# Recurrent layer and FP4 feed-forward layer on one core: the last two tiles' feed-forward middle in three column parts, and the end of four engines' programs as lists

## The chip, the core and the metric

The kernel runs on one core of one Trainium2 chip. The metric is the device time of one execution in microseconds (us). The kernel before took 566.85 us (median of 3 runs, 566.63 to 566.96).

## What is computed

The input x has 4 sequences of 2048 rows of 256 numbers, fp32. Two layers follow one another, each with a residual sum and a layer norm:

```python
# first layer: linear recurrence with a state of 16 numbers, then a norm with gamma and beta
xB = einsum('bsh,nh->bsn', x, B);  xD = einsum('bsh,oh->bso', x, D)
state = state @ A.T + xB_t                      # for every step t
out = layernorm(states @ C.T + xD) * gamma + beta
x = layernorm(x + out)
# second layer: gated feed-forward, 704 inner columns; every operand is quantized to FP4
# in blocks of 16 along its last dimension (scale = max|block| / 6) and dequantized
gate = fp4_linear(x, w_gate);  y = fp4_linear(x, w_up)
h = silu(gate) * y
x = layernorm(x + fp4_linear(h, w_down))
```

The output is x, again 4 x 2048 x 256.

## The kernel before

The 8192 rows are 64 tiles of 128 rows, numbered 0 to 63. In the code (h, m) is tile 8h + m. A prologue builds the states of the recurrence and quantizes the weights; then every tile goes through the same chain over five engines. Matmuls in fp32 are made of three passes over operands that are split into a high and a low part (`split_products`, line 1434), hence names such as htHi and htLo.

The chain of one tile, with the engine and the line: `layer` (TensorE, L1434 into yb), `mean_square` (ScalarE, L713), `ve1`, `pow1` (POOL, L534), `scale_gamma` and `add_x` (VectorE), `nm2`, `sq2`, `ve2`, `pow2`, `nr2`, `norm2` (L808); then the quantization of x1: `x_max` (L1062), `x_scale` (VectorE, L1067), `x_recip` (L1072), `x_norm` (POOL, L544), `x_abs` (ScalarE, L741), `x_sum`, `x_grid` (VectorE, L1077 and L1083), `x_scale` (POOL, L549), `x_turn` (TensorE transposes, L1460), `x_hi` (ScalarE, L754), `x_lo` (VectorE, L1088, writes xtLo). The gate and up products `gu0`, `gu1`, `gu2` (TensorE, L1434, into the three banks of gu, 512 + 512 + 384 columns) are next. The feed-forward middle is `silu_gate` (ScalarE, L758), `times_up` (VectorE, L1095, the product), `h_max` (L1099), `h_scale` and `h_recip` (L1104 and L1109), `h_norm` (POOL, L560), `h_abs` (ScalarE, L777), `h_sum` and `h_grid` (VectorE, L1126 and L1133), `h_scale` (POOL, L571 and L575), `h_turn` (six transposes, L1517), `h_hi` (ScalarE, L788), `h_lo` (VectorE, L1147), and the down projection `ffn_down` (17 matmuls, L1434, L1540, L1541). At the end of the chain stand `add_x1` (VectorE, L1154), `nm3` (L728), `sq3` (L735), `ve3` (L720), `pow3` (POOL, L534), `nr3` (L801), `norm3` (ScalarE, L817) and the store by SP.

Every engine runs its program in order, and semaphores tie them together: an instruction waits until a counter has reached its tile's number. The order of each program comes from `run`: a list of steps with lags, where step (op, lag) works in pass i of the loop on the tile i - lag:

```python
run(act, [(norm3, 11), (nm3, 9), (sq3, 9), (nr2, 3), (norm2, 3), (t_hi, 0), (h_hi, 7), (h_abs, 6),
          (silu_gate, 5), (nm2, 2), (x_hi, 4), (sq2, 2), (nr3, 10), (ve2, 2), (mean_square, 1),
          (x_abs, 3), (ve1, 1), (ve3, 9)], FILLED["act"])
run(dve, [(x_grid, 2), (scale_gamma, 0), (x_max, 1), (add_x, 0), (x_scale, 1), (h_lo, 5), (x_recip, 1),
          (h_sum, 4), (times_up, 3), (h_grid, 4), (x_lo, 2), (h_max, 3), (add_x1, 5), (h_scale, 3),
          (x_sum, 1), (h_recip, 3)], FILLED["dve"])
run(pe, [(h_turn, 6), (gu1, 4), (gu2, 4), (x_turn, 3), (layer, 0), (ffn_down, 6), (gu0, 3)], FILLED["pe"])
```

`run` writes a hardware loop over h = 2 to 7 and behind it the remaining passes (tiles that are still under way), in the same order. So the loop of each engine ends at another tile: ScalarE's last silu in the loop is that of tile 58, VectorE's last product in the loop that of tile 60, TensorE's last `gu0` in the loop that of tile 60.

At the end, tile 63 alone has its middle in two halves (`is_last`, `halves`, 384 + 320 columns) from `h_norm` on, and TensorE has four idle matmuls with the identity ahead of some steps (`unread(4, ...)`, L1293, twenty in all), which nothing reads. The down projections of the last five tiles write one half-bank, yb[:, 0:256], so each waits for the `add_x1` of the tile before.

## Time and profile before

| what | value |
| --- | --- |
| median of 3 runs | 566.85 us |
| the profiled execution | 566.68 us |
| its span, first to last instruction | 564.9 us |
| TensorE (PE) busy | 551.6 us, 98% |
| VectorE (DVE) busy | 518.0 us, 92% |
| POOL busy | 494.4 us, 88% |
| ScalarE (ACT) busy | 468.3 us, 83% |
| mean granted TensorE clock | 0.998 |

The profile is of one execution. Times of instructions are counted from the start of the span; the 1.8 us between span and execution lie around it. Busy times of TensorE count overlapping matmuls once. An instruction that is next in line overlaps the one before by about 0.1 us in the records. In the timelines the bracket behind a row gives the idle time of the engine before it and what ended it; the granted clock is a share of 2.4 GHz.

### The profile page before, as it was taken

The numbers are of one execution on the slowest core, as the hardware profiler recorded it, in microseconds if no ns is written. First come the engines' busy times: TensorE is split into PE (matmuls) and PEld (weight loads), VectorE is DVE, ScalarE is ACT, GpSimd is POOL, SyncE is SP. The second block draws the span as 40 slices with busy tenths as digits, with TensorE's granted clock in tenths as the row PEclk, the third lists the DMA queues.
The fourth block names the chain that finished last, engine by engine and source line by source line (L and its number), as shares of the span: only waits on it lengthen the run. The fifth ranks groups of instructions, "written<-read, shape, count | busy, mean of one in ns | idle before, by whom it ended". The sixth has DMA issues, their size and how long they took to land.

```text
span 564.9 us, 12830 instructions
## 1 busy us (share of the span) xinstructions
PE 551.6 (98%) x3751; PEld 495.0 (88%) x3751; DVE 518.0 (92%) x1241; ACT 468.3 (83%) x1415; POOL 494.4 (88%) x674
## 2 busy tenths in 40 slices
PE   9899999999999999999999999999999999999995
PEld 7577779999999999999999999999999999999894
DVE  4896799999999999999999999999999999999973
ACT  3557867889888998988889898888989888898756
POOL 2566887999999999999999999999999999998653
PEclk9999999999999999999999999999999999999999
DMA  8951000011121111111211111121111122100001
GB/s 291 383 182 30 5 24 24 22 41 47 56 61 60 52 60 58 49 50 59 59 52 56 58 50 50 59 59 55 54 59 49 50 59 59 56 22 19 20 20 46
DMA packets 35772, 36.25 MB, mean 64 GB/s; under 512 B 6752, under 2 KB 34464, under 8 KB 34720
## 3 DMA queue, kind: packets, MB, share of 16 engines
q1 hardware_dynamic: 35744, 35.90, 20.1%
q8 instruction: 14, 0.23, 0.2%
q14 instruction: 14, 0.11, 0.1%
HBM read 19.50 MB, written 8.39 MB: 49 GB/s over the span
## 4 chain that ended last, share of the span: by engine, by line
PE 90%; DVE 5%; ACT 2%; issue 1%; POOL 0%; POOLq 0%; DVEq 0%; ACTq 0%
PE gu L1434 41%; PE turned L1434 18%; PE yb L1434 8%; PE turned L1517 7%; PE turned L1460 2%; PE yb L1448 1%; PE grid L1293 1%; PE turned L1541 1%; PE turned L1540 1%; PE gu L1345 1%; PE yb L1345 1%; DVE scratch L1095 1%; DVE scratch L1133 1%; PE gu L1381 1%; PE turned L1381 1%
## 5 line engine op out<-in xcount | busy, mean ns | idle before, releaser
L1434 PE MATMUL gu<-wguHi,xtHi 128*128 128x512 f32 (+1 forms) x384 | 151.3, 394 | 0.4 <-DVE xtLo L1088 0.4
L1434 PE MATMUL gu<-wguLo,xtHi 128*128 128x512 f32 (+1 forms) x384 | 143.7, 374 | 0.0
L1434 PE MATMUL gu<-wguHi,xtLo 128*128 128x512 f32 (+1 forms) x384 | 143.7, 374 | 0.0
L560 POOL TENSOR_TENSOR scratch<-scratch 128x704 f32<-128x704 f32 x63 | 90.7, 1439 | 3.2 <-DVE scratch L1109 2.6
L571 POOL TENSOR_TENSOR scratch<-scratch 128x640 f32<-128x640 f32 x64 | 81.4, 1271 | 7.6 <-DVE scratch L1133 7.4
L1434 PE MATMUL turned<-wdHi,htHi 128*128 128x256 f32 x295 | 83.7, 284 | 0.0
L1434 PE MATMUL turned<-wdHi,htLo 128*128 128x256 f32 x295 | 83.6, 283 | 0.0
L1434 PEld LDWEIGHTS gu<-wguHi,xtLo 128*128 128x128 f32 x384 | 72.2, 188 | 12.3
L1434 PE MATMUL turned<-wdLo,htHi 128*128 128x256 f32 x295 | 82.6, 280 | 0.0
L1434 PEld LDWEIGHTS gu<-wguHi,xtHi 128*128 128x128 f32 x384 | 72.2, 188 | 9.9 <-DVE xtLo L1088 1.1
L1434 PEld LDWEIGHTS gu<-wguLo,xtHi 128*128 128x128 f32 x384 | 72.4, 189 | 8.2
L788 ACT CAST htHi<-turned 128x768 fp32r<-128x768 f32 x63 | 50.5, 801 | 28.5 <-PE turned L1517 28.5
L1147 DVE TENSOR_TENSOR htLo<-turned,htHi 128x768 fp32r<-128x768 f32 x63 | 60.3, 957 | 10.6 <-ACT htHi L788 4.2
L1099 DVE TENSOR_REDUCE gu<-scratch 128x44 f32<-128x704 f32 x64 | 56.5, 883 | 0.0
L1434 PEld LDWEIGHTS turned<-wdLo,htHi 128*128 128x128 f32 x295 | 56.2, 191 | 0.0
L1095 DVE TENSOR_TENSOR scratch<-scratch,gu 128x704 f32<-128x704 f32 x64 | 56.0, 875 | 0.1
L1133 DVE SCALAR_TENSOR_TENSOR scratch<-grid,scratch 128x704 f32<-128x704 f32 x63 | 55.7, 884 | 0.0
L1434 PEld LDWEIGHTS turned<-wdHi,htHi 128*128 128x128 f32 x295 | 55.4, 188 | 0.0
L1434 PEld LDWEIGHTS turned<-wdHi,htLo 128*128 128x128 f32 x295 | 55.2, 187 | 0.0
L534 POOL TENSOR_TENSOR rs<-ve2t,neg_half 128x1 f32<-128x1 f32 x64 | 35.4, 553 | 20.2 <-ACT ve2t L720 20.2
L1126 DVE SCALAR_TENSOR_TENSOR scratch<-grid,scratch 128x704 f32<-128x704 f32 x63 | 52.4, 831 | 0.2 <-ACT grid L777 0.2
L1517 PEld LDWEIGHTS turned<-ident,scratch 128*128 128x128 f32 x378 | 44.6, 140 | 8.9 <-POOL scratch L575 0.8
(225 smaller groups left out, 1679.7 us busy)
## 6 DMA issues: line engine op xcount, KB each, us to landing
xT<-in_L_attn_x_dram SPq DMA_DIRECT2D x8, 1024.0 KB, 9.9
scratch<-in_L_attn_x_dram SPq DMA_DIRECT2D x64, 128.0 KB, 2.4
out_dram<-scratch SPq DMA_DIRECT2D x64, 128.0 KB, 1.9
xtTile<-xT SPq DMA_DIRECT2D x48, 128.0 KB, 2.1
stTile<-statesHi SPq DMA_DIRECT2D x128, 8.0 KB, 1.7
stTile<-statesLo SPq DMA_DIRECT2D x64, 8.0 KB, 1.7
scratch<-in_L_ffn_w_down_dram SPq DMA_DIRECT2D x1, 704.0 KB, 10.3
scratch<-in_L_ffn_w_up_dram SPq DMA_DIRECT2D x1, 640.0 KB, 8.9
```

What stands on the lines that cost most here:

```text
L534: nc.gpsimd.tensor_tensor(dst[:, j:j + 1], src[:, j:j + 1], neg_half[:, :], ALU.pow).then_inc(signal, 1)
L560: nc.gpsimd.tensor_tensor(blocks(hx[:, m % 2, :]), blocks(hx[:, m % 2, :]), each_block(hRc[:, m % 4, :], FB), ALU.mult).then_inc(s_xnh, 1)
L571: nc.gpsimd.tensor_tensor(blocks(hq[:, m % 2, low:KD[-1]]), blocks(hq[:, m % 2, low:KD[-1]]), each_block(hSc[:, m % 4, low // BLOCK:KD[-1] ...
L788: nc.scalar.copy(htHi[:, m % 2, :, :].rearrange("p c k -> p (c k)"), ht).then_inc(s_hi, 1)
L1095: nc.vector.tensor_tensor(hx[:, m % 2, :], silu[:, m % 2, :], gu[:, FF:GU], ALU.mult).then_inc(s_h, 1)
L1099: nc.vector.tensor_reduce(amH, blocks(hx[:, m % 2, :]), AX_X, ALU.max, apply_absolute_value=True).then_inc(s_ham, 1)
L1126: nc.vector.scalar_tensor_tensor(out=v, in0=hm, scalar=LEAST, in1=v, op0=ALU.max, op1=ALU.add).then_inc(s_hsum, 1)
L1133: nc.vector.scalar_tensor_tensor(out=hq[:, m % 2, :], in0=hm, scalar=LEAST, in1=hx[:, m % 2, :], op0=ALU.max, op1=ALU.subtract, reverse1=T ...
L1147: nc.vector.tensor_tensor(htLo[:, m % 2, :, :].rearrange("p c k -> p (c k)"), ht, as_f32(htHi[:, m % 2, :, :]).rearrange("p c k -> p (c k) ...
L1345: ins = nc.tensor.transpose(to[:, q * P:(q + 1) * P], xT[:, h, t + q // KH, q % KH, :], ident[:, :])
L1434: ins = nc.tensor.matmul(to, l, r, start=(first and q == 0), stop=(last and q == len(passes) - 1))
L1517: ins = nc.tensor.transpose(ht[:, q * P:(q + 1) * P], rows, ident[:, :])
```

## The change

`run` no longer writes the passes behind the loop, except for SP. In their place stand lists of single calls for POOL, ScalarE, VectorE and TensorE, in an order of their own for each engine. The loops are unchanged. Tiles 62 and 63 have their feed-forward middle in three parts of 256, 256 and 192 columns: each part has its own gate and up columns in one bank of gu (`up_part`), and its own silu, product, maximum, scale, reciprocal, norm, abs, sum, grid, rescale, transposes (two each), hi, lo and down matmuls. The block maxima of the parts go to SBUF (hAm), where those of whole tiles stay in PSUM (amH). The norm of tiles 62 and 63 is one VectorE instruction (`norm_last`) in place of `nr3` and `norm3` on ScalarE. The twenty idle matmuls of the end become two. `sq3` of the last tiles writes its squares, which nothing reads, to xTile. The halves of tile 63 are gone.

```diff
-            for i in range(last):
+            for i in range(last if eng is nc.sync else 0):
                 step(HALVES, i, False)
...
+        SPLIT = 2
+        FIRST_SPLIT = TILES - SPLIT
+        PARTS = ((0, 2 * P), (2 * P, 4 * P), (4 * P, FF))
+
+        def is_split(tile):
+            return tile >= FIRST_SPLIT
+
+        def part(tile, k):
+
+            return tile + 1 + 2 * (tile - FIRST_SPLIT) + k
+
+        def all_parts(tile):
+
+            return part(tile, len(PARTS) - 1) if is_split(tile) else tile + 1
...
+        hm_parts = [grid[:, 0:2 * P], grid[:, 512:512 + 2 * P], grid[:, 2 * P:FF - 2 * P]]
+        ht_parts = [turned[:, 512:512 + 2 * P], turned[:, 0:2 * P], turned[:, 512 + 2 * P:512 + 4 * P]]
+
+        def gu_part(k):
+
+            a, b = PARTS[k]
+            return gu[:, 512 * k:512 * k + 2 * (b - a)].rearrange("p (g f) -> p g f", g=2)
...
+            def norm_part(h, m, k):
+                tile, (a, b), (bl, n) = h * CHUNK + m, PARTS[k], part_blocks(k)
+                pool.wait_ge(s_amh, part(tile, k))
+                nc.gpsimd.tensor_tensor(blocks(hx[:, m % 2, a:b]), blocks(hx[:, m % 2, a:b]),
+                                        each_block(hRc[:, m % 4, bl], n), ALU.mult).then_inc(s_xnh, 1)
+
+            def rescale_part(h, m, k):
+                tile, (a, b), (bl, n) = h * CHUNK + m, PARTS[k], part_blocks(k)
+                pool.wait_ge(s_gh, part(tile, k))
+                last = k == len(PARTS) - 1
+                nb = REST // BLOCK
+                if last:
+                    b, bl, n = KD[-1], slice(bl.start, bl.stop - nb), n - nb
+                ins = nc.gpsimd.tensor_tensor(blocks(hq[:, m % 2, a:b]), blocks(hq[:, m % 2, a:b]),
+                                              each_block(hSc[:, m % 4, bl], n), ALU.mult)
+                if last:
+                    ins = nc.gpsimd.tensor_tensor(
+                        hTail[:, m % 2, :].rearrange("p (a b k) -> p a b k", a=2, k=BLOCK),
+                        blocks(hq[:, m % 2, KD[-1]:FF]).unsqueeze(1).to_broadcast([P, 2, nb, BLOCK]),
+                        each_block(hSc[:, m % 4, FB - nb:], nb).unsqueeze(1).to_broadcast([P, 2, nb, BLOCK]), ALU.mult)
+                ins.then_inc(s_qh, 1)
...
+            pow3(6, 6)
+            x_scale(7, 4)
+            h_norm(7, 2)
+            x_norm(7, 5)
+            pow2(7, 6)
+            pow3(6, 7)
+            h_scale(7, 2)
+            pow3(7, 0)
+            pow1(7, 7)
+            h_norm(7, 3)
...
+                    squares = junk
+                    if buf is x1 and isinstance(h, int) and h >= HALVES - 2:
+                        act.wait_ge(s_xb, TILES)
+                        squares = xTile[:, m % RING, :]
+                    nc.scalar.activation(squares, buf[:, m % ring, :], ACT.Square, bias=mean[:, j:j + 1],
...
+            def silu_part(h, m, k):
+                tile, (a, b) = h * CHUNK + m, PARTS[k]
+                act.wait_ge(s_gate, part(tile, k))
+                nc.scalar.activation(silu[:, m % 2, a:b], gu_part(k)[:, 0, :], ACT.Silu).then_inc(s_silu, 1)
+
+            def abs_part(h, m, k):
+                tile, (a, b) = h * CHUNK + m, PARTS[k]
+                act.wait_ge(s_xnh, part(tile, k))
+                if k == 2:
+                    act.wait_ge(s_gh, part(tile, 0))
+                elif is_split(tile - 1):
+                    act.wait_ge(s_gh, part(tile - 1, 2 if k == 0 else 1))
+                else:
+                    act.wait_ge(s_gh, tile)
+                nc.scalar.activation(hm_parts[k], hx[:, m % 2, a:b], ACT.Abs, scale=MAGIC).then_inc(s_mh, 1)
+
+            def hi_part(h, m, k):
+                tile = h * CHUNK + m
+                act.wait_ge(s_t, part(tile, k))
+                nc.scalar.copy(htHi[:, m % 2, 2 * k:2 * k + 2, :].rearrange("p c k -> p (c k)"),
+                               ht_parts[k]).then_inc(s_hi, 1)
...
+            nr2(7, 5)
+            norm3(6, 5)
+            norm2(7, 5)
+            nm3(6, 7)
+            nm3(7, 0)
+            sq3(6, 7)
+            sq3(7, 0)
+            nr3(6, 6)
+            h_hi(7, 1)
+            nm2(7, 6)
+            norm3(6, 6)
+            sq2(7, 6)
+            h_abs(7, 2)
+            ve2(7, 6)
+            x_abs(7, 5)
+            x_hi(7, 4)
+            ve3(6, 7)
+            nr2(7, 6)
+            mean_square(7, 7)
+            ve3(7, 0)
+            nr3(6, 7)
+            ve1(7, 7)
+            norm3(6, 7)
+            norm2(7, 6)
+            silu_gate(7, 3)
+            nm3(7, 1)
...
+            def times_up_part(h, m, k):
+                tile, (a, b) = h * CHUNK + m, PARTS[k]
+                dve.wait_ge(s_silu, part(tile, k))
+                nc.vector.tensor_tensor(hx[:, m % 2, a:b], silu[:, m % 2, a:b], gu_part(k)[:, 1, :],
+                                        ALU.mult).then_inc(s_h, 1)
...
+            def scale_part(h, m, k):
+                tile, (bl, n) = h * CHUNK + m, part_blocks(k)
+                dve.wait_ge(s_ham, part(tile, k))
+                nc.vector.tensor_scalar(hSc[:, m % 4, bl], hAm[:, m % 4, bl], SIXTH, MIN_SCALE, ALU.mult,
+                                        ALU.max).then_inc(s_hsc, 1)
...
+            def grid_part(h, m, k):
+                tile, (a, b) = h * CHUNK + m, PARTS[k]
+                dve.wait_ge(s_t, part(tile - 2, k) if is_split(tile - 2) else tile - 1)
+                dve.wait_ge(s_hsum, part(tile, k))
+                nc.vector.scalar_tensor_tensor(out=hq[:, m % 2, a:b], in0=hm_parts[k], scalar=LEAST,
+                                               in1=hx[:, m % 2, a:b], op0=ALU.max, op1=ALU.subtract,
+                                               reverse1=True).then_inc(s_gh, 1)
...
+            def norm_last(h, m):
+                r = m % RING
+                dve.wait_ge(s_st[r], done_dma(h, m - RING))
+                dve.wait_ge(s_pow3, done(h, m))
+                nc.vector.tensor_scalar(outTile[:, r, :], x1[:, m, :], nm3t[:, m:m + 1], rs3[:, m:m + 1], ALU.add,
+                                        ALU.mult).then_inc(s_out, 1)
...
-            def is_ending(h, m):
-
-                return isinstance(h, int) and h * CHUNK + m >= TILES - 3
-
             def h_turn(h, m):
                 tile = h * CHUNK + m
-                if is_ending(h, m) and tile >= TILES - 2:
-                    pe.wait_ge(s_silu, TILES)
-                    unread(4, gu)
...
-                if is_ending(h, m):
-                    unread(4, to)
...
+            def up_part(h, m, k):
+                tile, (a, b) = h * CHUNK + m, PARTS[k]
+                if k == 0:
+                    pe.wait_ge(s_xlo, done(h, m))
+                if is_split(tile - 1):
+                    pe.wait_ge(s_h, part(tile - 1, k))
+                else:
+                    pe.wait_ge([s_silu, s_h, s_hsc][k], tile)
+
+                def columns(w, c):
+                    return w[:, c, :].rearrange("p (g f) -> p g f", g=2)[:, :, a:b]
+
+                split_products(gu_part(k), [((xtHi[:, m % 2, c, :], xtLo[:, m % 2, c, :]),
+                                             (columns(wguHi, c), columns(wguLo, c))) for c in range(KH)]).then_inc(s_gate, 1)
...
+            def turn_part(h, m, k):
+                tile = h * CHUNK + m
+                if k == 2:
+                    pe.wait_ge(s_lo, part(tile, 0))
+                elif is_split(tile - 1):
+                    pe.wait_ge(s_lo, part(tile - 1, 2 if k == 0 else 1))
+                else:
+                    pe.wait_ge(s_lo, tile)
+                pe.wait_ge(s_xlo, TILES)
+                pe.wait_ge(s_qh, part(tile, k))
+                for q in range(2):
+                    row = KD[2 * k + q]
+                    rows = hq[:, m % 2, row:row + P] if row + P <= FF else hTail[:, m % 2, :]
+                    ins = nc.tensor.transpose(ht_parts[k][:, q * P:(q + 1) * P], rows, ident[:, :])
+                ins.then_inc(s_t, 1)
+
+            def down_part(h, m, k):
+                tile, to = h * CHUNK + m, down_bank(h, m)
+                if k == 0:
+                    pe.wait_ge(s_x1p, TILES)
+                    pe.wait_ge(s_r, tile)
+                    unread(1, to)
+                pe.wait_ge(s_lo, part(tile, k))
+                pairs = range(2 * k, 2 * k + 2) if k < 2 else range(4, NKD - 1)
+                split_products(to, [((htHi[:, m % 2, q, :], htLo[:, m % 2, q, :]), (wdHi[:, q, :], wdLo[:, q, :]))
+                                    for q in pairs], first=k == 0, last=False)
...
+            turn_part(7, 6, 0)
+            turn_part(7, 6, 1)
+            ffn_down(7, 5)
+            turn_part(7, 6, 2)
+            down_part(7, 6, 0)
+            down_part(7, 6, 1)
+            turn_part(7, 7, 0)
+            down_part(7, 6, 2)
+            turn_part(7, 7, 1)
+            down_part(7, 7, 0)
+            turn_part(7, 7, 2)
+            down_part(7, 7, 1)
+            down_part(7, 7, 2)
```

The order of instructions shows the two places. First ScalarE, behind the loop. Before, from `h_hi` of tile 57 to `ve1` of tile 63; names are those of the tensors, `gu` in L758 is the input of silu of tile 59, `yb,ms` in L713 that of `mean_square` of tile 63:

```order
L788 CAST htHi<-turned 128x768 [waits s_t]
L777 ACTIVATE grid<-scratch 128x704 [waits s_gh,s_xnh]
L758 ACTIVATE scratch<-gu 128x704 [waits s_gate]
L728 ACTIVATE nm2t<-sum 128x1 [waits s_x1p]
L754 CAST xtHi<-turned 128x256 [waits s_tx]
L735 ACTIVATE scratch,ss<-scratch,nm2t 128x256 [waits s_nm2]
L801 ACTIVATE nr3t<-nm3t,rs 128x1 [waits s_pow3]
L720 ACTIVATE ve2t<-ss,eps 128x1 [waits s_sq2]
L713 ACTIVATE yb,ms<-yb 128x256 [waits s_y]
L741 ACTIVATE scratch<-scratch 128x256 [waits s_xnx]
L720 ACTIVATE ve1t<-ms,eps 128x1 [waits s_sq1]
```

In the change the same place of ScalarE's program, from `x_abs` of tile 61 (L802) over `mean_square` of tile 63 (L770) to the silu of tile 59 (L819):

```order
L802 ACTIVATE scratch<-scratch 128x256 [waits s_xnx]
L815 CAST xtHi<-turned 128x256 [waits s_tx]
L777 ACTIVATE ve3t<-ss,eps 128x1 [waits s_sq3]
L868 ACTIVATE nr2t<-nm2t,rs 128x1 [waits s_pow2]
L770 ACTIVATE yb,ms<-yb 128x256 [waits s_y]
L777 ACTIVATE ve3t<-ss,eps 128x1 [waits s_sq3]
L868 ACTIVATE nr3t<-nm3t,rs 128x1 [waits s_pow3]
L777 ACTIVATE ve1t<-ms,eps 128x1 [waits s_sq1]
L886 ACTIVATE scratch<-scratch,nr3t,rs 128x256 [waits s_nr3,s_st3]
L877 ACTIVATE scratch<-scratch,nr2t,rs 128x256 [waits s_nr2,s_out]
L819 ACTIVATE scratch<-gu 128x704 [waits s_gate]
```

The silu of tile 59 stood second behind `h_hi` of tile 57 and now stands behind `mean_square` and `ve1` of tile 63 and two norms.

The second place is VectorE's program around `add_x1` of tile 61. Before, from `h_max` of tile 63 on:

```order
L1099 TENSOR_REDUCE gu<-scratch 128x44 [waits s_h]
L1154 SCALAR_TENSOR_TENSOR scratch,sum<-yb,scratch 128x256 [waits s_dn]
L1104 TENSOR_SCALAR scratch<-gu 128x44 [waits s_ham]
L1109 RECIPROCAL scratch<-scratch 128x44 [waits s_hsc]
L1147 TENSOR_TENSOR htLo<-turned,htHi 128x768 [waits s_hi]
L1118 SCALAR_TENSOR_TENSOR scratch<-grid,scratch 128x384 [waits s_mh]
```

In the change, from the three maxima of tile 63 (L1308) to `add_x1` of tile 61 (L1295), with the scales from SBUF (L1314) and `lo_part` (L1340) of tile 62 among them:

```order
L1308 TENSOR_REDUCE scratch<-scratch 128x16 [waits s_h] x2
L1302 TENSOR_TENSOR scratch<-scratch,gu 128x192 [waits s_silu]
L1314 TENSOR_SCALAR scratch<-scratch 128x16 [waits s_ham]
L1340 TENSOR_TENSOR htLo<-turned,htHi 128x256 [waits s_hi]
L1320 RECIPROCAL scratch<-scratch 128x16 [waits s_hsc]
L1340 TENSOR_TENSOR htLo<-turned,htHi 128x256 [waits s_hi]
L1314 TENSOR_SCALAR scratch<-scratch 128x16 [waits s_ham]
L1308 TENSOR_REDUCE scratch<-scratch 128x12 [waits s_h]
L1320 RECIPROCAL scratch<-scratch 128x16 [waits s_hsc]
L1314 TENSOR_SCALAR scratch<-scratch 128x12 [waits s_ham]
L1295 SCALAR_TENSOR_TENSOR scratch,sum<-yb,scratch 128x256 [waits s_dn]
```

`add_x1` of tile 61 stood right behind `h_max` of tile 63; now part-wise work of tiles 62 and 63 stands in front of it.

## Rows read from the trace of the kernel before

**Rows 1.** Stretches of the end: length, busy us of PE, PEld, DVE, ACT, POOL; clock, DMA, GB/s.

```profile
545.60:562.50 16.90, 12.48 (x104) 11.95 (x102) 8.46 (x19) 10.65 (x34) 7.64 (x12) 1.00 0.11 38
562.50:565.00 2.50, 0.00 (x0) 0.00 (x0) 0.00 (x0) 0.00 (x0) 0.00 (x0) 0.52 0.17 59
```

**Rows 2.** Timeline of ScalarE: start us, us, engine, line, operation, out<-in, [idle before].

```profile
515.54 0.74 ACT L758 ACTIVATE scratch<-gu 128x704 f32<-128x704 f32 x1
...
517.94 0.37 ACT L713 ACTIVATE yb<-yb 128x256 f32<-128x256 f32 x1
...
518.63 0.28 ACT L720 ACTIVATE ve1t<-ms,eps 128x1 f32<-128x1 f32 x1
518.82 0.28 ACT L720 ACTIVATE ve3t<-ss,eps 128x1 f32<-128x1 f32 x1
519.01 0.59 ACT L817 ACTIVATE scratch<-scratch,nr3t,rs 128x256 f32<-128x256 f32 x1
...
521.72 0.80 ACT L788 CAST htHi<-turned 128x768 fp32r<-128x768 f32 x1 [0.57 <-PE turned L1517]
```

**Rows 3.** Timeline of VectorE at the same time.

```profile
514.54 0.30 DVE L1067 TENSOR_SCALAR xSc<-xAm 128x16 f32<-128x16 f32 x1
...
516.74 0.88 DVE L1095 TENSOR_TENSOR scratch<-scratch,gu 128x704 f32<-128x704 f32 x1
...
518.33 0.42 DVE L1088 TENSOR_TENSOR xtLo<-turned,xtHi 128x256 fp32r<-128x256 f32 x1
```

**Rows 4.** Timeline of TensorE: first gate matmuls of tile 60 and of tile 61.

```profile
519.47 0.40 PE L1434 MATMUL gu<-wguHi,xtHi 128*128 128x512 f32 x1
...
526.39 0.50 PE L1434 MATMUL gu<-wguHi,xtHi 128*128 128x512 f32 x1
```

**Rows 5.** Timeline of POOL: h_norm of tile 58, x_scale of tile 60, pow3 of tile 54.

```profile
513.37 1.44 POOL L560 TENSOR_TENSOR scratch<-scratch 128x704 f32<-128x704 f32 x1
514.77 0.62 POOL L549 TENSOR_TENSOR scratch<-scratch,xSc 128x256 f32<-128x256 f32 x1
515.35 0.55 POOL L534 TENSOR_TENSOR rs<-ve3t,neg_half 128x1 f32<-128x1 f32 x1
```

**Rows 6.** Timeline of all engines at 528.5: h_norm of tile 60, x_scale of tile 63.

```profile
528.56 1.44 POOL L560 TENSOR_TENSOR scratch<-scratch 128x704 f32<-128x704 f32 x1 [0.70 <-DVE scratch L1109]
...
529.12 0.92 DVE L1067 TENSOR_SCALAR xSc<-xAm 128x16 f32<-128x16 f32 x1
```

**Rows 7.** Timeline of TensorE, from the gate matmuls of tile 63.

```profile
540.95 0.49 PE L1434 MATMUL gu<-wguHi,xtHi 128*128 128x512 f32 x1 [0.15 <-DVE xtLo L1088]
...
542.46 0.81 PE L1517 MATMUL turned<-ident,scratch 128*128 128x128 f32 x6
...
545.57 1.05 PE L1293 MATMUL yb<-ident 128*128 128x128 f32 x8
546.38 0.37 PE L1434 MATMUL yb<-wdHi,htHi 128*128 128x256 f32 x1
...
548.50 1.05 PE L1293 MATMUL gu<-ident 128*128 128x128 f32 x8
```

**Rows 8.** Timeline of all engines behind the last matmul: last down matmul to last norm.

```profile
558.79 0.28 PE L1541 MATMUL yb<-wdLo,htLo 128*128 128x256 f32 x1
...
559.11 0.42 DVE L1154 SCALAR_TENSOR_TENSOR scratch<-yb,scratch 128x256 f32<-128x256 f32 x1 [1.92 <-PE yb L1541]
...
560.86 0.55 POOL L534 TENSOR_TENSOR rs<-ve3t,neg_half 128x1 f32<-128x1 f32 x1 [1.74 <-ACT ve3t L720]
561.44 0.29 ACT L801 ACTIVATE nr3t<-nm3t,rs 128x1 f32<-128x1 f32 x1 [0.15 <-POOL rs L534]
561.83 0.60 ACT L817 ACTIVATE scratch<-scratch,nr3t,rs 128x256 f32<-128x256 f32 x1
```

**Rows 9.** The scale instructions of VectorE by line: duration in ns, minimum/median/maximum.

```profile
L1067 DVE TENSOR_SCALAR xSc<-xAm x64: 169/298/918, 56.7 to 529.1; 128x16 f32<-128x16 f32 x64
...
L1104 DVE TENSOR_SCALAR scratch<-gu x64: 183/198/201, 70.3 to 549.1; 128x44 f32<-128x44 f32 x64
```

323 lines of the change are left out of this document (231 added, 92 removed).

## The prediction

> **What bounds the kernel now.** I read the table of stretches first. Until the last gate/up matmul, TensorE is busy all the time and sets the pace; in the last 17 us before the final store it is busy for 12.48 of 16.90 us, and its granted clock stays at 1.00, the upper level of 2.4 GHz [rows 1]. So two places count: the seam where the loop gives way to the straight end, and the end itself. Tiles are numbered 0 to 63; (7, m) is tile 56 + m.
>
> **The seam.** The timelines of the engines around 514 to 522 us come next. ScalarE computes the silu of tile 59 at 515.54, right behind its h_abs [rows 2]. Two instructions that stand in the last passes of the loops, which the change doesn't touch, use it: VectorE's gate/up product of tile 59 at 516.74, and TensorE's next gate matmuls, of tile 60, at 519.47 [rows 3, 4]. VectorE is in order, so behind that product stand the grid step of tile 58 and the subtraction that makes xtLo of tile 60 at 518.33 [rows 3], and TensorE needs that too. In the new ScalarE list silu of tile 59 stands 16 places behind h_hi(57), behind mean_square(63), ve3, nr3, ve1, norm3(55) and norm2(62).
>
> *Low price.* mean_square(63) waits for TensorE's layer matmuls, so it can't start before 517.94 [rows 2]. Its two instructions give way after 0.39. Three one-column instructions follow 0.19 apart (the starts 518.63, 518.82, 519.01) [rows 2]: 518.90. norm3 and norm2 take 0.60 each and overlap by 0.1 [rows 8]: silu starts at 519.9 and ends at 520.64, and VectorE's product starts at 520.65 instead of 516.74. xtLo of tile 60 was ready 2.01 us after that product's start (518.33 + 0.42 - 516.74) [rows 3]: 522.7, against TensorE's start at 519.47 now. **TensorE stands still for 3.2 us.**
>
> *High price.* The small multiplication x_scale(61) on VectorE starts at 514.54 and takes 0.30 [rows 3]. A later one of the same form took 0.92: it started at 529.12, while POOL's 704-column h_norm ran from 528.56 for 1.44, and both ended at 530.0 [rows 6]; over all tiles it takes 0.17 to 0.92 [rows 9]. So a running POOL instruction holds it up. The new POOL list has pow3(54) and x_scale(60) ahead of h_norm(58), 0.55 + 0.62 long [rows 5]: h_norm(58) starts at 514.4 instead of 513.37 and ends at 515.85, just over the start of x_scale(61), which then ends 1.0 us later than now. x_norm(61), and x_abs(61) in front of mean_square(63), follow it, so mean_square(63) starts at 518.75 and the stop is 4.0 us. The two starts are 0.14 us apart, so this could miss; I take it as more likely than not.
>
> The Trainium skill states the same lock as a rule, in "SBUF — State Buffer", section "Who interferes with whom": a Vector instruction in a two-port mode and a GpSimd one exclude each other for the whole instruction. By that rule the high price holds; the 0.92 us row agrees.
>
> *A second delay.* h_hi(58) now stands behind nr3(56), sq3(57) and norm3(56), and nr3(56) waits for pow3(56), which stands on POOL behind h_scale(58). From the end of h_scale(58): 0.55 + 0.2 + 0.6 + 0.5 = 1.8, against 0.07 + 0.82 for TensorE's six transposes [rows 7]: 0.9 late, where h_hi(58) starts at 521.72 behind idle time [rows 2]. Everything from there to the gate matmuls of tile 61 (526.39, 4.67 later) [rows 4] hangs in a row. Lateness at tile 61: 4.1 to 4.9. Tiles 62 and 63 have 0.28 and 0.15 of slack at most, so at the gate matmuls of tile 63 (540.95 now) [rows 7] it is 3.7 to 4.9; **I take +4.5**. Nothing hides it: TensorE has no other instruction that it may run there, since its order is fixed.
>
> **The end.** From the gate matmuls of tile 63 to the end of the last norm it takes 562.43 - 540.95 = 21.5 us now [rows 7, 8]: the 704-wide chain of one tile (product, maximum, h_norm, h_abs, sum, grid, h_scale, transposes, h_hi, h_lo) can't overlap with itself. In three parts TensorE gets its work earlier. Its work in the new order: 4.62 for gate/up with the transposes of tile 61 (540.95 to 545.57); three down projections, each of 2.12 (546.38 to 548.50) [rows 7], 6.4; six pairs of transposes at 0.22, 1.3; two single fillers in place of twenty, 0.5; 0.2 until the last result lands. Sum 13.0. Waits that stay: down of tile 62 writes the PSUM half-bank that add_x1(61) reads, and on VectorE 28 instructions of 0.29 on the mean (16 columns take 0.17, 256 take 0.42, 704 take 0.88 [rows 3, 9]), 8.1 us, stand between xtLo of tile 63 and add_x1(61), so TensorE, ready at 7.4, waits 1.0; add_x1(62) 0.4; hand-offs from transposes over ScalarE and VectorE to the down parts of tile 63 0.7. So the last down result is at 15.1 instead of 18.1 (559.07 - 540.95) [rows 7, 8].
>
> Behind it add_x1, nm3, sq3, ve3 and pow3 stay: 559.11 to 561.41 is 2.30 [rows 8]. norm_last, one VectorE instruction, takes the place of nr3 and norm3 (to 562.43, 1.02). Its form is not in the trace; the bounds are 0.17 (16 columns) and 0.42 (256 columns, two tensors) [rows 3, 9]; I take 0.42, the row of its width. ve3(63) also loses the nr3 in front of it, 0.18. New tail: 15.1 + 0.05 + 2.30 - 0.18 + 0.03 + 0.42 = 17.7, against 21.5. **I take -3.7.** Bounds: no wait at all gives -5.8; waits and hand-offs twice as long give -1.6.
>
> The six scale parts now read hAm in SBUF, not amH in PSUM. The form from PSUM takes 0.18 to 0.20 in every case; the one from SBUF 0.17 to 0.92 [rows 9]. At most two of them lie where POOL is in a long instruction and VectorE is the one waited for; 0.2 to 0.9 in all, within the waits above. By the Trainium skill's rule named above all six may stall, each for the rest of POOL's instruction, 0.4 us on the mean; the sum would then be at the slow bound, as in the rival of dear hand-offs.
>
> The other edits are free: sq3 writes its unused squares to xTile (its wait on all 64 add_beta is past), norm2 waits for a store-side norm done eight tiles earlier, SP's program keeps its order, and the last store still follows the last norm by 2.5 us.
>
> **Sum.** +4.5 - 3.7 = +0.8 on the profiled execution of 566.68 us, 567.5. It lies 0.17 under the median of the three runs (566.85), so I forecast **567.7 us**. 0.2%, 1.1 us, is about what a measurement of this kernel can tell from no change.
>
> **The rivals.**
> - *Slower: TensorE's clock falls in the pause.* Its idle times in the end stay under 1 us so far, with the clock at 1.00; in the last stretch, from 3.4 us after its last matmul (559.07) on, it is 0.52, the lower level of 1.2 GHz, nearly throughout [rows 1, 8]. The new pause is 3.2 to 4.0. If it falls, matmuls run at 1.2 GHz, and if that lasts for as much work as the pause was long, this takes up to twice as long: +1.7 to +3.4, 569.4 to 571. For it: the pause is by far the longest of the run. Against: it is only just long enough. Chance 0.1. The Trainium skill has an idle TensorE throttled to half its clock ("TensorE: Matmul & The Clock Gate", Part 1), which the row after the last matmul bears out.
> - *Slower: the hand-offs of the parts are dear.* VectorE runs some 55 small instructions in 18 us; decides if each part's turn costs 0.1 more and the locks hit. Then the end gives back only 1.6 to 2.3: +2.2 to +2.9, about 569.2. For it: VectorE is the busiest engine there. Chance 0.15.
> - *Faster: the stop at its low price, the parts nearly without waits.* +3.7 - 5.5 = -1.8, 565.0; it decides if x_scale(61) comes through before h_norm(58), and add_x1(61) isn't late. Against: VectorE's 8.4 us are counted. Chance 0.13.
> - *The port never matters.* Low price, usual waits: 3.7 - 3.9 = -0.2, 566.6. Chance 0.12.
> - That the change doesn't do what it says is excluded by the order of instructions, which shows parts and the late silu.
>
> **The numbers.** The forecast's own case (+0.3 to +1.6) has 0.5, of which 0.1 lies over the 1.1 us. Slower: 0.1 + 0.15 + 0.1 = 0.35. Faster by over 1.1 us: most of 0.13, 0.1. Within: 0.55. The range 565.3 to 569.4 leaves out the better half of the fast case, most of the clock case and a little of the hand-offs, 0.2 together.
>
> **What would show it.** In the profile after: TensorE idle for 3 to 4 us at about 520, ended by xtLo of tile 60 (line 1252); VectorE idle as long before the product at line 1259, released by the silu at line 819; x_scale (line 1231) at 1.1 us or more near 514.5; the gate matmuls of tile 63 near 545.5; last down result 15 us later; norm_last 0.3 to 0.5. I am wrong if TensorE has no such pause, if the granted clock falls at 520 to 527, or if the end from tile 63's gate matmuls is shorter than 16.5 or longer than 19 us.

## The result: 568.05 us, 0.3% more than before

The changed kernel takes **568.05 us** (median of 22 runs, 567.75 to 570.7); the kernel before took 566.63 us beside it (22 runs). The ratio is 1.003, with a 95% interval of 1.0018 to 1.0041. The forecast was 567.7 us, in a range of 565.3 to 569.4, with the most chance on no measurable difference; the difference of 1.4 us lies just over the 1.1 us named there. The profiled execution took 567.94 us and spans 566.0 us. Two executions far off the others, at a low granted clock, are left out of every median and ratio: one of the kernel before (778 us) and one of experiment 3 (901.75 us).

**Where the time went.** The times of one kernel scatter by 3 to 4 us (565.71 to 570.07 for the kernel before). Much of it lies ahead of the seam: in the profiles of this document pow1(62) starts anywhere from 511.85 to 514.85. I therefore measure from one instruction that no edit touches and that lies ahead of the new lists: POOL's pow1(62), the last instruction of its loop (line 534 before, 542 after). It starts at 512.63 in the profile of before and at 512.06 in that of after.

| us from the start of pow1(62) | before | after | difference |
|---|---|---|---|
| gate matmuls of tile 60 | 6.84 | 10.82 | +3.98 |
| of tile 61 | 13.76 | 19.38 | +5.62 |
| of tile 62 | 21.15 | 26.89 | +5.74 |
| of tile 63 | 28.32 | 33.76 | +5.44 |
| end of the last norm | 49.80 | 51.52 | +1.72 |

So the seam, the place where the loop gives way to the lists, costs 5.4 us at tile 63 (4.5 taken in the prediction), and the end gives back 3.7 (3.7 taken).

**The seam after.** The timeline of POOL and VectorE (start us, us, engine, line, operation, out<-in, in brackets the idle time before and what ended it):

```profile
512.06 0.73 POOL L542 TENSOR_TENSOR rs<-ve1t,neg_half 128x1 f32<-128x1 f32 x1
512.76 0.64 POOL L542 TENSOR_TENSOR rs<-ve3t,neg_half 128x1 f32<-128x1 f32 x1
513.37 0.62 POOL L557 TENSOR_TENSOR scratch<-scratch,xSc 128x256 f32<-128x256 f32 x1
513.95 1.39 POOL L562 TENSOR_TENSOR scratch<-scratch 128x704 f32<-128x704 f32 x1
...
513.98 1.40 DVE L1231 TENSOR_SCALAR xSc<-xAm 128x16 f32<-128x16 f32 x1
515.29 0.94 DVE L1288 TENSOR_TENSOR htLo<-turned,htHi 128x768 fp32r<-128x768 f32 x1
...
520.81 0.89 DVE L1259 TENSOR_TENSOR scratch<-scratch,gu 128x704 f32<-128x704 f32 x1 [3.67 <-ACT scratch L819]
521.61 0.88 DVE L1283 SCALAR_TENSOR_TENSOR scratch<-grid,scratch 128x704 f32<-128x704 f32 x1
522.41 0.41 DVE L1252 TENSOR_TENSOR xtLo<-turned,xtHi 128x256 fp32r<-128x256 f32 x1
```

pow3(54) and x_scale(60) now stand ahead of h_norm(58), which starts at 513.95. VectorE's x_scale(61) starts 0.03 us later and takes 1.40 us, until POOL is done; it took 0.30 in [rows 3]. The product of tile 59 stands 3.67 us for the silu, and xtLo of tile 60 goes behind it, where [rows 3] have no idle time. ScalarE and TensorE at the same place:

```profile
520.04 0.73 ACT L819 ACTIVATE scratch<-gu 128x704 f32<-128x704 f32 x1
...
519.46 0.28 PE L1778 MATMUL turned<-wdLo,htLo 128*128 128x256 f32 x1
522.88 0.50 PE L1695 MATMUL gu<-wguHi,xtHi 128*128 128x512 f32 x1 [3.15 <-DVE xtLo L1252]
...
523.45 0.40 PE L1695 MATMUL gu<-wguHi,xtLo 128*128 128x512 f32 x1
...
524.50 0.63 PE L1695 MATMUL gu<-wguHi,xtLo 128*128 128x512 f32 x1
524.93 1.48 PE L1762 MATMUL turned<-ident,scratch 128*128 128x128 f32 x6
```

The silu runs at 520.04 (515.54 in [rows 2]), and TensorE has its pause of 3.15 us. Behind it, matmuls of one shape go from 0.40 to 0.63 us, and six transposes take 1.48 (0.81 in [rows 7]). The table of stretches says why (length; busy us of PE, PEld, DVE, ACT, POOL; granted clock; DMA):

```profile
520.00:524.00 4.00, 1.12 (x4) 0.96 (x5) 3.19 (x8) 0.78 (x3) 1.42 (x2) 0.97 0.09 33
524.00:527.00 3.00, 3.00 (x11) 2.49 (x10) 2.46 (x9) 2.03 (x6) 3.00 (x5) 0.50 0.00 0
527.00:528.00 1.00, 1.00 (x5) 0.79 (x4) 0.72 (x1) 1.00 (x3) 0.45 (x1) 0.93 0.37 131
528.00:545.80 17.80, 17.48 (x112) 15.56 (x111) 17.27 (x38) 13.44 (x36) 11.97 (x16) 1.00 0.07 23
545.80:561.00 15.20, 13.46 (x93) 11.82 (x91) 12.73 (x46) 9.20 (x31) 9.29 (x18) 1.00 0.05 18
```

**The clock fell to its lower level of 1.2 GHz**, but not in the pause: it fell 0.8 us after TensorE had started again and stayed down from about 523.7 to 527.1. That was the rival to which I gave 0.1.

**The end after.** TensorE is busy for 13.46 us between 545.8 and 561.0, with VectorE close behind (12.73). What stays of waits, and the tail:

```profile
545.82 0.39 PE L1695 MATMUL gu<-wguHi,xtHi 128*128 128x512 f32 x1
...
554.13 0.46 PE L1554 MATMUL yb<-ident 128*128 128x128 f32 x2 [0.95 <-DVE scratch L1295]
...
560.49 0.28 PE L1824 MATMUL yb<-wdLo,htLo 128*128 128x256 f32 x1
...
560.81 0.42 DVE L1295 SCALAR_TENSOR_TENSOR scratch<-yb,scratch 128x256 f32<-128x256 f32 x1
563.17 0.41 DVE L1348 TENSOR_SCALAR scratch<-scratch,nm3t,rs 128x256 f32<-128x256 f32 x1 [1.93 <-POOL rs L542]
```

From the gate matmuls of tile 63 (545.82) to the end of the last norm (563.58) it is 17.76 us, against 21.5 in [rows 7, 8]; the filler ahead of tile 62's down projection waits 0.95 us for add_x1(61), and norm_last takes 0.41. The six scale parts are in one row of the trace (ns, minimum/median/maximum); one, at 552.65, was clearly held up:

```profile
L1314 DVE TENSOR_SCALAR scratch<-scratch x6: 124/166/532, 543.0 to 553.5; 128x16 f32<-128x16 f32 x4, 128x12 f32<-128x12 f32 x2
```

It ends with the POOL instruction that was running, and stands in a row of VectorE instructions without idle time, four places ahead of add_x1(61), for which TensorE waits:

```profile
552.54 0.62 POOL L578 TENSOR_TENSOR scratch<-scratch 128x256 f32<-128x256 f32 x1 [0.74 <-DVE scratch L1320]
552.65 0.53 DVE L1314 TENSOR_SCALAR scratch<-scratch 128x16 f32<-128x16 f32 x1
...
553.56 0.41 DVE L1295 SCALAR_TENSOR_TENSOR scratch<-yb,scratch 128x256 f32<-128x256 f32 x1
```

### The profile page after: what moved, and what is told of

Same layout as the page of the kernel before. It is cut to its first block, busy times and chain, and to the rows that moved or that the text cites. A ratio compares the mean times of both kernels' runs of the same rounds, so it can differ in the third digit from the quotient of the medians.

```text
span 566.0 us, 12820 instructions
## 1 busy us (share of the span) xinstructions
PE 549.3 (97%) x3715; PEld 491.6 (87%) x3715; DVE 521.6 (92%) x1268; ACT 468.0 (83%) x1421; POOL 495.8 (88%) x680
## 4 chain that ended last, share of the span: by engine, by line
PE 88%; DVE 7%; ACT 2%; issue 1%; POOL 0%; POOLq 0%; DVEq 0%
PE gu L1695 40%; PE turned L1695 18%; PE yb L1695 8%; PE turned L1762 7%; PE turned L1721 2%; PE yb L1709 1%; PE turned L1778 1%; PE grid L1554 1%; PE turned L1777 1%; PE gu L1606 1%; PE yb L1606 1%; DVE htLo L1288 1%; DVE scratch L1259 1%; DVE scratch L1283 1%; PE gu L1642 1%
## 5 line engine op out<-in xcount | busy, mean ns | idle before, releaser
L562 POOL TENSOR_TENSOR scratch<-scratch 128x704 f32<-128x704 f32 x62 | 89.2, 1439 | 3.5 <-DVE scratch L1273 3.0
L567 POOL TENSOR_TENSOR scratch<-scratch 128x640 f32<-128x640 f32 x62 | 79.5, 1282 | 5.9 <-DVE scratch L1283 5.6
L1259 DVE TENSOR_TENSOR scratch<-scratch,gu 128x704 f32<-128x704 f32 x62 | 54.2, 875 | 4.0 <-ACT scratch L819 3.7
L1283 DVE SCALAR_TENSOR_TENSOR scratch<-grid,scratch 128x704 f32<-128x704 f32 x62 | 54.7, 882 | 0.0
L1263 DVE TENSOR_REDUCE gu<-scratch 128x44 f32<-128x704 f32 x62 | 54.7, 883 | 0.0
L1278 DVE SCALAR_TENSOR_TENSOR scratch<-grid,scratch 128x704 f32<-128x704 f32 x62 | 51.5, 831 | 0.0
```

The lines of the kernel that those rows point to most:

```text
L562: nc.gpsimd.tensor_tensor(blocks(hx[:, m % 2, :]), blocks(hx[:, m % 2, :]), each_block(hRc[:, m % 4, :], FB), ALU.mult).then_inc(s_xnh, 1)
L567: nc.gpsimd.tensor_tensor(blocks(hq[:, m % 2, 0:KD[-1]]), blocks(hq[:, m % 2, 0:KD[-1]]), each_block(hSc[:, m % 4, 0:KD[-1] // BLOCK], KD[ ...
L1259: nc.vector.tensor_tensor(hx[:, m % 2, :], silu[:, m % 2, :], gu[:, FF:GU], ALU.mult).then_inc(s_h, 1)
L1263: nc.vector.tensor_reduce(amH, blocks(hx[:, m % 2, :]), AX_X, ALU.max, apply_absolute_value=True).then_inc(s_ham, 1)
L1278: nc.vector.scalar_tensor_tensor(out=v, in0=hm, scalar=LEAST, in1=v, op0=ALU.max, op1=ALU.add).then_inc(s_hsum, 1)
L1283: nc.vector.scalar_tensor_tensor(out=hq[:, m % 2, :], in0=hm, scalar=LEAST, in1=hx[:, m % 2, :], op0=ALU.max, op1=ALU.subtract, reverse1=T ...
```

## The experiments

**1. The silu back in its place.** One line moved:

```diff
             h_abs(7, 2)
+            silu_gate(7, 3)
...
             norm2(7, 6)
-            silu_gate(7, 3)
```

> The changed kernel with one line moved: the silu of tile 59 stands right behind h_abs(58) in ScalarE's list, where it stood before the change. Theory (the late silu is the whole cost of the seam, the parts give back some 3.6 us): no pause of TensorE at 520, no fall of its granted clock at 524, the end from the gate matmuls of tile 63 still 17.5 to 18.2 us; 563.0 to 564.7 us, likeliest 564.1, so 2 to 3.5 us under the kernel before. Rival (the written-out lists lose time elsewhere too, the silu is only a part): 565.5 to 567. Rival (the seam is harmless and the end gives back only what it gave): no change against the changed kernel, 567.5 to 568.5.

Measured: 563.72 us, ratio to before 0.9943 (0.9921 to 0.9966). The pause is gone, the clock stays at 1.00, and the end is as long as in the changed kernel, 17.78 us. From pow1(62) the last norm ends at 47.13, 2.67 us earlier than before and 4.39 earlier than in the changed kernel. **One misplaced instruction cost 4.4 us.** It is not the whole seam: of the 3.7 us that the end gives back, 2.67 are left, because the gate matmuls of tile 63 still come 1.03 us later than before (29.35 against 28.32). Experiment 6 looks for that rest. The stretches of this kernel (same columns):

```profile
520.00:524.00 4.00, 4.00 (x23) 3.22 (x21) 3.53 (x13) 3.21 (x9) 3.52 (x5) 1.00 0.19 66
524.00:528.00 4.00, 3.67 (x25) 3.27 (x25) 4.00 (x10) 3.61 (x12) 3.10 (x5) 1.00 0.00 0
```

**2. The seam alone.** The kernel before with only that silu late (in ScalarE's tail, from the point where sq3(56) is done):

```diff
             for i in range(last):
+                if eng is nc.scalar and i < 2:
+                    for op, lag in ops:
+                        if (op is not ops[8][0] or i > 0) and 0 <= CHUNK * HALVES + i - lag < TILES:
+                            op(HALVES, i - lag)
+                        if i == 1 and op is ops[2][0]:
+                            ops[8][0](HALVES, -5)
+                    continue
                 step(HALVES, i, False)
```

> The kernel before with one step moved: the silu of tile 59 waits in ScalarE's program until behind mean_square(63) and the third-norm steps that follow it (3 instructions of one column, a norm3 and a sq3 between), about where the changed kernel has it; POOL's order, the two halves and the fillers of the end stay. Theory: TensorE stands for 3.0 to 3.6 us before the gate matmuls of tile 60, its granted clock falls to 0.5 behind that as in the changed kernel, nothing is given back: 3.7 to 4.8 us over the kernel before, 570.3 to 571.5. If the clock did not fall: 569.8 to 570.4. Rival (something else makes the pause, POOL's order or the parts' waits): less than 1.5 us over.

Measured: 572.8 us (571.39 to 573.07, 6 runs), ratio 1.0091 (1.0064 to 1.0117), more than the 570.3 to 571.5 expected. The profiled execution took 571.52, 55.04 from pow1(62) to the end: +5.24, over the 4.8 expected. The pause and the clock came as expected:

```profile
522.64 0.50 PE L1441 MATMUL gu<-wguHi,xtHi 128*128 128x512 f32 x1 [3.44 <-DVE xtLo L1095]
```

```profile
522.60:524.00 1.40, 1.35 (x6) 1.05 (x6) 1.40 (x5) 0.00 (x0) 1.40 (x3) 1.00 0.00 0
524.00:527.00 3.00, 3.00 (x12) 2.65 (x11) 2.56 (x9) 1.25 (x2) 2.99 (x4) 0.50 0.00 0
```

Gate to gate of tiles 60 and 61 takes 8.55 us instead of 6.92, +1.63, the same as in the changed kernel (8.56). I had priced the fall too low: with the clock down TensorE is busy through the whole stretch (3.00 of 3.00 us), so all that it loses is lost to the kernel.

**3. POOL's h_norm(58) 0.6 earlier.**

```diff
             pow3(6, 6)
+            h_norm(7, 2)
             x_scale(7, 4)
-            h_norm(7, 2)
```

> The changed kernel with POOL's h_norm(58) ahead of x_scale(60), behind pow3(54). It then starts 0.6 earlier, at 513.35, and so ends 0.6 earlier, and VectorE's x_scale(61), which starts at 513.98, is held up for 0.6 us less: 0.80 instead of 1.40 us. Theory (POOL's instruction holds it up until its end, and all that follows hangs on that): 0.5 to 0.7 us less than the changed kernel, 567.4; if the pause of 2.55 us is then too short for the clock to fall, 0.6 to 1.0 less again, 566.6. Rival (x_scale is slow for another reason, or the pause hangs on ScalarE's list alone): no change, 567.9 to 568.3.

Measured: 568.2 us, median of 11 runs from 566.78 to 570.03; ratio to before 1.0013 (0.9992 to 1.0035). The times can't tell it from the changed kernel (567.4 was expected). The trace is clearer: h_norm(58) starts at 513.16, and

```profile
513.76 0.81 DVE L1231 TENSOR_SCALAR xSc<-xAm 128x16 f32<-128x16 f32 x1
```

The gate matmuls of tile 60 are at 10.24 from pow1(62), 0.58 earlier than in the changed kernel, and the last norm ends 0.56 earlier (50.96). So the hold-up is passed on one for one (x_scale(61) ends 0.60 earlier), **shown** by the traces; in experiment 6 (a) the same move brings tile 60 forward by 0.49. My side remark was wrong: the pause stayed at 3.18, since everything ahead of it moved too, and the clock fell as before.

**4. Keeping TensorE busy in the pause**, first with 20 unread products, then with 12. TensorE's last pass is written out; the last product gives the signal of the down projection whose half bank it uses, so that add_x1(57) waits for it:

```diff
...
+                    if k == 0 and isinstance(tile, int) and tile == TILES - 4:
+                        unread(12, turned[:, 768:1024], signal=s_dn)
                     if k == 0:
                         pe.wait_ge(s_xlo, done(h, m))
...
-                nc.tensor.matmul(to, htLo[:, m % 2, NKD - 1, :], wdLo[:, NKD - 1, :], start=False,
-                                 stop=True).then_inc(s_dn, 1)
+                ins = nc.tensor.matmul(to, htLo[:, m % 2, NKD - 1, :], wdLo[:, NKD - 1, :], start=False,
+                                       stop=True)
+                if not isinstance(tile, int) or tile != TILES - 7:
+                    ins.then_inc(s_dn, 1)
```

> The changed kernel with 20 unread products of 128 columns (0.14 us each, 2.8 in all) on TensorE in the pause ahead of the gate matmuls of tile 60, in the half bank of the down projection of tile 57, whose signal the last of them gives; for this TensorE's last loop pass is written out. Theory (the clock falls because TensorE stood still, and the slow stretch of 3.4 us behind the pause delays everything after it): granted clock 1.00 throughout, gate matmuls of tile 60 at the same time as in the changed kernel, those of tile 63 0.6 to 1.2 earlier; 567.0 to 567.5. Rival (the slow stretch is covered, since h_hi(58) is late behind nr3(56), sq3(57) and norm3(56) anyway): clock 1.00, but 567.8 to 568.2. Rival (the written-out pass costs as much in fetching its code): a new idle time before, and 568 or more.

> As the kernel with 20 unread products in the pause, with 12: in that run each product took two instructions and 0.23 us together, 4.63 for all, so they ran 1.0 us over the pause. 12 take 2.8 and end ahead of xtLo of tile 60. Theory (the fall of the clock costs 1.5 us, since from the gate matmuls of tile 60 to those of tile 61 it is 8.56 us in the changed kernel and was 7.01 with the clock at 1.00): the gate matmuls of tile 60 at the changed kernel's time, those of tile 61 7.0 us later, 566.3 to 566.8. Rival (the 7.01 was short only because tile 60 had been held up by the fillers, so that ScalarE was ahead): 7.9 or more there, 567.3 to 567.9.

> The changed kernel with TensorE's last loop pass written out and nothing else, as in the kernels with unread products. Theory: writing it out costs nothing, 567.7 to 568.4 with the clock's fall as in the changed kernel. Rival: fetching the straight code costs 0.3 us or more, 568.3 to 569, and what the unread products give is larger by that.

With 20 the products took 4.63 us, not 2.8, and held tile 60 up by 1.0: that test mixes two things, although the clock stayed at 1.00. 12 fit the pause:

```profile
521.99 2.84 PE L1558 MATMUL turned<-ident 128*128 128x128 f32 x24
525.37 0.50 PE L1701 MATMUL gu<-wguHi,xtHi 128*128 128x512 f32 x1 [0.54 <-DVE xtLo L1256]
```

```profile
525.30:529.00 3.70, 3.63 (x19) 3.02 (x20) 3.26 (x11) 1.78 (x6) 3.70 (x5) 1.00 0.00 0
```

Measured: 567.55 us for 12 products (ratio to before 1.0006, 0.9982 to 1.003), 568.01 for 20, 568.36 for the written-out pass alone (1.0029, 1.0008 to 1.0049); the intervals overlap, so what follows rests on the traces. From pow1(62), 12 products have tile 60 at 10.82, as the changed kernel, and the end at 50.87, 0.65 earlier. The written-out pass alone has 10.82 and 51.51, so it costs nothing in the trace. The rival in the expectation for 12 products held: with the clock up, gate to gate of tiles 60 and 61 is 7.88, not 7.0. **The fall takes 1.6 us of TensorE's time, and 0.65 of the kernel's**; the rest runs at the same time as the second delay of the prediction, which is 7.88 - 6.92 = 0.96 us long with the clock up.

**5. norm_last given back to ScalarE.**

```diff
             ve3(7, 7)
+            nr3(7, 6)
+            norm3(7, 6)
+            nr3(7, 7)
+            norm3(7, 7)
...
-            norm_last(7, 6)
...
-            norm_last(7, 7)
```

> The changed kernel with the last norm of tiles 62 and 63 given back to ScalarE: nr3 and norm3 behind ve3(63) for each, in place of VectorE's norm_last. Theory (norm_last is 0.41 against 0.30 + 0.60 with their hand-off, and nr3(62) and norm3(62) stand in front of tile 63's, 0.2 behind pow3(63)): the end longer by 0.6 to 0.8 us, 568.4 to 568.9. Rival (the last store is bound by something else): no change, 567.8 to 568.1.

Measured: 569.17 us (568.4 to 568.9 expected), ratio 1.0052 (1.0025 to 1.0078), against 1.003 (1.0018 to 1.0041) of the changed kernel; the intervals overlap, and the trace decides. From the gate matmuls of tile 63 to the last norm's end it is 18.40 us instead of 17.76: **norm_last is worth 0.64**. By accident this execution showed more:

```profile
523.46 0.50 PE L1697 MATMUL gu<-wguHi,xtHi 128*128 128x512 f32 x1 [3.18 <-DVE xtLo L1256]
524.97 0.82 PE L1764 MATMUL turned<-ident,scratch 128*128 128x128 f32 x6
528.61 0.41 PE L1723 MATMUL turned<-ident,scratch 128*128 128x128 f32 x2 [0.36 <-DVE htLo L1292]
```

The pause was as long as in the changed kernel, yet the transposes take 0.82, the clock stayed at 1.00 (522 to 530), and the gate matmuls of tile 63 came at 33.09, as with the products (33.09) and 0.67 earlier than in the changed kernel. So a pause of 3.2 us brings the clock down in some executions, in four of the five profiled ones that have it.

**6. What the second delay is.** On top of experiment 1: h_norm(58) moved as in 3 (a); then h_hi(58) ahead of nr3(56), sq3(57) and norm3(56) (b); or pow1(63) ahead of pow3(56) on POOL (c); or both (d):

```diff
+            pow1(7, 7)
             pow3(7, 0)
-            pow1(7, 7)
...
             nm3(7, 1)
+            h_hi(7, 2)
             nr3(7, 0)
...
-            h_hi(7, 2)
```

> The kernel with the silu of tile 59 moved back, and POOL's h_norm(58) ahead of x_scale(60) as well. Theory (in the kernel with the silu alone x_scale(61) still takes 1.40 us, h_lo(57) behind it is late and TensorE's transposes of tile 60 wait 0.42 us for it): x_scale(61) 0.8, that wait gone, gate matmuls of tile 60 0.4 to 0.6 earlier, which the tiles after it keep in part: 0.1 to 0.5 us under the kernel with the silu alone, 562.8 to 563.4. Rival (x_scale(60), now later, delays x_abs(60) and with it the transposes): no gain or a loss, 563.4 to 564.

> The kernel with the silu and h_norm(58) moved, and h_hi(58) ahead of nr3(56), sq3(57) and norm3(56) in ScalarE's list as well. Theory (the second delay is h_hi(58) standing behind these, and behind pow3(56) through nr3(56): in the kernel with the two moves TensorE's transposes of tile 61 wait 0.37 us for h_lo(58), and gate to gate of tiles 60 and 61 is 7.89 us against 6.92 before the change): h_hi(58) starts 0.9 us earlier, the wait of 0.37 goes, gate to gate 7.0 to 7.2; 0.3 to 0.8 us less in all, 562.4 to 563.2. Rival (what is moved behind h_hi(58), the third norm's steps, then delays h_abs(59) and the silu of tile 60, or VectorE is the one that is late): gate to gate 7.6 or more, no gain, 563.2 to 564.

> The kernel with the silu and h_norm(58) moved, and POOL's pow1(63) ahead of pow3(56) as well. In that kernel two engines meet at h_lo(58): h_hi(58) ends at 523.36 and VectorE, which has stood 0.44 us for pow1(63), is there at 523.36 too. Theory (both rows behind the second delay are of equal length, so either alone gives nothing): VectorE no longer waits for pow1(63), but pow3(56) comes 0.7 later, and with it nr3(56) and h_hi(58); gate to gate of tiles 60 and 61 8.3 to 8.7 us instead of 7.89. Rival (only VectorE is late): 7.4 to 7.6, and 0.4 less in all.

> The same with h_hi(58) ahead of nr3(56), sq3(57) and norm3(56) too. Theory of the two rows: both are shorter, by 0.9 on ScalarE and by 0.44 to 0.7 on VectorE, gate to gate 7.2 to 7.5 us instead of 7.89 (7.97 with h_hi(58) alone), and half of it or more stays to the end. Rival (what is put behind h_hi(58) holds up h_abs(59) and the silu of tile 60, as when h_hi(58) alone was moved): 7.6 or more.

The kernel before took 566.2 to 567.0 us (median) beside these runs, and the times of (a) to (d) can't be told apart. All columns but the first in us from the start of pow1(62); "x_scale" is the end of x_scale(62), "h_norm" that of h_norm(59):

| | time, us | gate 60 | h_norm | x_scale | h_lo(58) starts | gate 61 | last norm's end |
|---|---|---|---|---|---|---|---|
| before | 566.63 | 6.84 | 9.78 | 9.81 | 9.92 | 13.76 | 49.80 |
| silu alone | 563.72 | 7.48 | 11.05 | 11.08 | 11.10 | 14.94 | 47.13 |
| (a) | 563.9 | 6.99 | 10.98 | 11.01 | 11.04 | 14.88 | 47.04 |
| (b) | 563.99 | 7.00 | 11.00 | 11.02 | 10.94 | 14.97 | 47.31 |
| (c) | 564.68 | 7.00 | 10.99 | 11.01 | 11.66 | 15.50 | 47.71 |
| (d) | 564.51 | 7.00 | 10.99 | 11.02 | 10.94 | 14.99 | 47.33 |

In (a) tile 60 gains the 0.49 us that the hold-up of x_scale(61) cost, and tile 61 doesn't keep it. In (b) h_hi(58) runs earlier and nothing follows it. (c) came as its theory has it: nr3(56) waits 1.35 us for pow3(56), and h_hi(58) is the late one, gate to gate 8.50. (d) gave nothing either, where I expected 7.2 to 7.5. The two columns in the middle say why: **x_scale(62) ends 0.02 to 0.03 us after h_norm(59), in every row**, whatever its start. In (a) and in (d):

```profile
521.94 1.39 POOL L562 TENSOR_TENSOR scratch<-scratch 128x704 f32<-128x704 f32 x1
...
523.07 0.29 DVE L1231 TENSOR_SCALAR xSc<-xAm 128x16 f32<-128x16 f32 x1
523.39 0.96 DVE L1288 TENSOR_TENSOR htLo<-turned,htHi 128x768 fp32r<-128x768 f32 x1
```

```profile
522.24 1.39 POOL L562 TENSOR_TENSOR scratch<-scratch 128x704 f32<-128x704 f32 x1
...
522.84 0.82 DVE L1231 TENSOR_SCALAR xSc<-xAm 128x16 f32<-128x16 f32 x1
523.58 0.94 DVE L1288 TENSOR_TENSOR htLo<-turned,htHi 128x768 fp32r<-128x768 f32 x1
```

VectorE starts this instruction 0.52 us earlier in (d), from pow1(62), and ends it at the same moment. So POOL holds VectorE up here, and the new POOL list has h_norm(59) behind pow3(56), where it was ahead of it: 1.2 us later than before, of which 0.7 is the later start of h_scale(58) and the rest pow3(56). (b), (c) and (d) leave that sum as it is. Whether putting h_norm(59) ahead of pow3(56) and pow1(63) cures it was not tried.

**7. A search over the lists.** The lists of ScalarE, VectorE and POOL with many small moves; TensorE's order as it is, the silu in its old place:

```diff
             ve2(7, 6)
-            x_abs(7, 5)
+            ve3(6, 7)
+            norm3(6, 6)
+            ve3(7, 0)
             x_hi(7, 4)
-            ve3(6, 7)
...
```

> The changed kernel with the silu of tile 59 moved back and some forty small changes of place in the lists of ScalarE, VectorE and POOL, each by one to six places, the order of TensorE kept: a search for whether the rest of the lists hides as much as the silu did. Theory (the silu was the one misplaced instruction, the rest is near what TensorE's and VectorE's work allow): 562.2 to 563.6, at most 1.5 us under the kernel with the silu alone. Rival (the lists hold much more): under 562.

Measured: 563.69 us (6 runs; 562.2 to 563.6 expected), ratio 0.9956 (0.994 to 0.9971). In the trace it is 46.44 us from pow1(62) to the end, 0.69 under experiment 1, which the times can't tell apart. The silu is the one misplaced instruction of weight that this search found. Its trace agrees with experiment 6: h_norm(59) ends at 10.59, 0.4 us earlier than in (a), x_scale(62) at 10.62, and the gate matmuls of tile 61 come at 14.36; but much else moved there, so this is a hint and no proof. Experiment 1, a one-line change, takes 0.6% less than the kernel before and some 0.8% less than the changed one; 7 can't be told from it.

## Why the prediction held, point by point

The total held, 567.7 against 568.05, in part by luck. As a difference the forecast was +0.85 and the measurement +1.42; a kernel before that came out 0.22 lower this time (566.63 for 566.85) brings the totals closer. Inside the sum the clock's fall stood at nothing and cost 0.65; had the second delay not covered most of it, the total would have missed by 1 us more. The terms:

- **The stop of TensorE.** Low price 3.2, high price 4.0, the high one taken as more likely than not: 3.98, by the path named, x_scale(61) held up for 1.40 us by an h_norm(58) that had started 0.03 us before. The margin was 0.14 in the prediction, so it was a near thing; it was 0.02 or 0.03 in all six profiles that have this POOL order, and the hold-up 1.40 each time. Experiment 3 shows the hold-up passed on one for one. The rule of the Trainium skill named there ("SBUF — State Buffer", section "Who interferes with whom") agrees with the x_scale instructions of these traces: in the profiles of before and after, 59 of the 64 met a running 704-column POOL instruction, and each ended 0.02 to 0.04 us behind it. The traces show the hold-up, not the mode of the instruction. They also correct a reading: the 0.30 us of [rows 3], which I took as the free duration, was held up as well, since it ended at 514.84 and h_norm(58) at 513.37 + 1.44 = 514.81 [rows 5].
- **The second delay.** 0.9 predicted, 0.96 measured with the clock up (experiments 4 and 5); the size was right, and the path only one of two. I had "nr3(56) waits for pow3(56), which stands on POOL behind h_scale(58)"; that row exists, as (c) shows. But pow3(56) stands ahead of h_norm(59) too, h_norm(59) holds up VectorE's x_scale(62), and h_lo(58) stands behind that. It is the step of the high price once more, one tile later, and I had looked for it at one place only.
- **Lateness at tile 63.** +4.5 taken, 3.7 to 4.9 as its bounds; it is 4.77 without the fall of the clock (33.09 - 28.32, twice), and 5.44 with it.
- **The clock.** This is the step that failed: "Against: it is only just long enough. Chance 0.1." By the prediction's own signs it is wrong here ("if the granted clock falls at 520 to 527"). The clock fell in four of five profiled executions with such a pause. The Trainium skill's rule that an idle TensorE is throttled to half its clock ("TensorE: Matmul & The Clock Gate", Part 1) agrees with the four in which it fell. The rival's price, 1.7 to 3.4 us, was wrong the other way. It is not even what its own premise gives: matmuls at half speed for as long as a pause of 3.2 to 4.0 us, or for that much work, would be 1.6 to 4.0. And it took for granted that nothing else is late in that time. The slow stretch, 523.7 to 527.1, cost TensorE 1.6, and 0.96 of that lay under the second delay: 0.65 in all. Two errors, of the chance and of the price, met in a total that held. In experiment 2, which has no such cover, the full 1.63 is paid.
- **The end.** 17.7 predicted, 17.76 measured; last down result at +15.1 (560.77 - 545.82 = 14.95 measured), the wait for add_x1(61) 1.0 (0.95), norm_last 0.42 (0.41). The 15.1 came out of two misses that cancel: TensorE's work was 13.4 us (13.0 taken) and its waits 1.5 (2.1 taken). Experiment 1 has the same end (17.78) behind a seam without the stop. What norm_last brings against nr3 and norm3 is 0.64 by experiment 5.
- **The scale parts.** At most two to be held up, 0.2 to 0.9 in all: one, for some 0.4; the prediction's other reading, that all six stall, did not come. It stands in front of add_x1(61), so up to 0.4 of TensorE's 0.95 us wait is this hold-up. What it costs the kernel is open: in experiment 7 that wait is 0.32 us and the end no shorter (17.81), and no run puts the maxima back into PSUM.
- **The sum.** Terms 5.44 - 3.72 = +1.72 in the profiled executions, against +0.8; the difference is the clock (0.67) and 0.27 on the seam. In the medians it is +1.4.
- The sign was given half right: 0.35 for slower by more than the bound, 0.55 for within. With a chance for the clock like four in five, slower would have been the likelier of the two.
